# A gated delta-rule decoder layer on one Trainium2 core: output weights and roots earlier on GpSimd, the copy of the inverse on GpSimd, first odd units in other banks

## What is computed

```python
mixed = hidden_states @ w_qkv
z = (hidden_states @ w_z).reshape(B, S, HV, DV)
...
y = jax.lax.conv_general_dilated(x, conv_w, window_strides=(1,), padding=[(KCONV - 1, 0)], ...)
mixed = jax.nn.silu(y).transpose(0, 2, 1)
...
def step(Sm, inp):
    q_, k_, v_, g_, b_ = inp
    Sm = Sm * jnp.exp(g_)[..., None, None]
    kv = jnp.einsum('bhk,bhkv->bhv', k_, Sm)
    delta = (v_ - kv) * b_[..., None]
    Sm = Sm + jnp.einsum('bhk,bhv->bhkv', k_, delta)
    o = jnp.einsum('bhk,bhkv->bhv', q_, Sm)
    return (Sm, o)
...
og = o * jax.nn.silu(z)
var = jnp.mean(og * og, axis=-1, keepdims=True)
on = og * jax.lax.rsqrt(var + EPS) * norm_w
return on.reshape(B, S, VAL_DIM) @ w_out
```

## Time and profile before

| | us |
|---|---|
| median of three runs | 2256.93 |
| lowest and highest run | 2249.43, 2257.33 |
| profiled execution, its own time | 2255.11 |
| span of its instructions | 2253.2 |
| TensorE busy | 2091.6 (93%) |
| VectorE busy | 1711.3 (76%) |
| ScalarE busy | 1512.7 (67%) |
| GpSimd busy | 904.1 (40%) |

### The profile page before, as it was taken

The page is one execution under the profiler, slowest core; times in us unless marked ns, Lnnn a source line. Parts: engine busy times, 40 slices in busy tenths (PEclk is TensorE's granted clock), DMA queues, the critical chain, the costliest instruction groups (busy, mean ns, idle before and its releaser), DMA issues.

```text
span 2253.2 us, 49295 instructions
## 1 busy us (share of the span) xinstructions
PE 2091.6 (93%) x18636; PEld 1716.1 (76%) x18636; DVE 1711.3 (76%) x2944; ACT 1512.7 (67%) x3585; POOL 904.1 (40%) x714
## 2 busy tenths in 40 slices
PE   4659999999999999999999999999988899999998
PEld 4448888888888888888888888887776476666776
DVE  6789797887879788787977978787325777767665
ACT  4547777777777777777777677775767666565632
POOL 1534454444445445445535534532333123213232
PEclk8779999999999999999999999998999999999999
DMA  3432322322232332233233222212243012322232
GB/s 77 94 73 48 89 44 72 63 64 67 55 85 46 72 75 49 68 60 80 52 70 72 48 70 56 75 34 56 58 137 133 1 66 76 104 94 73 91 136 85
DMA packets 274633, 161.56 MB, mean 72 GB/s; under 512 B 209352, under 2 KB 246752, under 8 KB 269280
## 3 DMA queue, kind: packets, MB, share of 16 engines
q1 hardware_dynamic: 274400, 158.41, 27.6%
HBM read 122.43 MB, written 35.91 MB: 70 GB/s over the span
## 4 chain that ended last, share of the span: by engine, by line
issue 36%; POOL 26%; PE 23%; DVE 8%; ACT 4%; DMA 2%; SPq 2%; POOLq 0%; DVEq 0%; ACTq 0%
POOL SM L577 5%; POOL EB L493 5%; POOL Q L555 5%; PE ps L1739 4%; POOL SZ L579 3%; PE ps L1347 3%; POOL EB L497 3%; PE ps L1349 3%; PE ps L1348 3%; POOL WL L471 2%; POOL SM L585 2%; PE ps L1660 1%; ACT SC L856 1%; PE ps L1651 1%; PE ps L1480 1%
## 5 line engine op out<-in xcount | busy, mean ns | idle before, releaser
L909 DVE SCALAR_TENSOR_TENSOR A<-ps,CW,A 128x508 f32<-128x508 f32 (+2 forms) x768 | 515.9, 734 | 55.3 <-ACT A L671 50.1
L572 POOL TENSOR_SCALAR SM<-SM 128x8 f32<-128x8 f32 x64 | 12.6, 196 | 813.8 <-ACT DL L690 813.8
L1480 PE MATMUL ps<-WO,DL 128*128 128x256 f32 x1008 | 244.5, 394 | 39.5 <-POOL WO L484 24.5
L1480 PEld LDWEIGHTS ps<-WO,DL 128*128 128x128 f32 x1008 | 189.7, 194 | 74.5 <-POOL WO L484 26.4
L1347 PE MATMUL ps<-XH,WH 128*128 128x512 f32 x512 | 221.5, 433 | 26.7 <-DVE A L909 25.8
L1127 DVE TENSOR_TENSOR SZ<-SZ,ps 128x512 f32<-128x512 f32 x128 | 87.7, 687 | 201.5 <-PE ps L1514 201.4
L1349 PE MATMUL ps<-XH,WL 128*128 128x512 f32 x512 | 206.4, 403 | 0.0
L1348 PE MATMUL ps<-XL,WH 128*128 128x512 f32 x512 | 205.2, 401 | 0.0
L690 ACT ACTIVATE DL<-SZ 128x128 f32<-128x128 f32 x512 | 152.4, 298 | 38.5 <-PE ps L1514 28.8
L856 ACT ACTIVATE SC<-ps,A 128x128 f32<-128x128 f32 x512 | 141.7, 386 | 51.5 <-DVE A L1252 50.7
L1112 DVE TENSOR_TENSOR BP<-ps,EB 128x512 f32<-128x512 f32 x256 | 158.3, 681 | 3.3 <-ACT EB L665 3.3
(11 more groups left out here) (225 smaller groups left out, 5556.1 us busy)
## 6 DMA issues: line engine op xcount, KB each, us to landing
EB<-decay_rows SPq DMA_DIRECT2D x128, 256.0 KB, 4.7
WE<-expert_halves SPq DMA_DIRECT2D x32, 1024.0 KB, 5.1
x_blocks<-BP SPq DMA_DIRECT2D x256, 32.0 KB, 1.7
X<-x_blocks SPq DMA_DIRECT2D x16, 512.0 KB, 6.5
tt_blocks<-TI SPq DMA_DIRECT2D x16, 512.0 KB, 2.6
tn_blocks<-TM SPq DMA_DIRECT2D x16, 512.0 KB, 2.6
TTF<-tt_blocks SPq DMA_DIRECT2D x256, 32.0 KB, 1.9
expert_halves<-BP SPq DMA_DIRECT2D x8, 1024.0 KB, 5.8
```

Source lines behind the costliest of these rows:

```text
L909: dve.scalar_tensor_tensor(acc, ps(i, 0, [[128, 4], [1, 128 - s]]), at(CW, tile * 4 + 3 - s, [[1, 1]]), acc, ALU.mult, ALU.add).then_inc(s ...
L1480: t = pe.matmul(ps(7 - i, b * 256, [[1, 256]]), at(on_buf(k), (4 * i + 2 * b + v) * 128, [[1, 128]]), at(WO, v * 256, [[1, 256]]), start=( ...
```

## The change

Four things are changed.

1. `load_wo` and `scale_wo` of the next key head are called in ticks 4j (k % 4 == 3) and no longer in ticks 4j+1: on SyncE behind `load_rows`, on GpSimd behind `decay` and ahead of the norm of unit m.
2. The root of the keys' norms (L585, now L570) stands ahead of that norm as well, in the same tick as before.
3. The copy `TM<-TI` is taken off ScalarE and made by GpSimd's `tensor_copy` behind `decay`, in the same ticks 4j+3. The title's "moved within GpSimd's tick" holds for the root; the copy comes from another engine.
4. Units 1, 3, 5 and 7 project into banks 4 and 5. A projection in the first ticks waits for the taps of the unit two before, ScalarE does `kq_tap3(n + 1)` ahead of the `Silu` of unit n for n < 6, and three waits are adapted (the first projection on `ab`, `kq_tap3(6)` on the unit two before, the first transposes of values on the taps of unit 7).

```diff
@@ -217,6 +217,9 @@
         def kq_buf(n):
             return A2 if n < 6 and n % 2 else A1
 
+        def kq_bank(n):
+            return 4 if n < 8 and n % 2 else 0
+
@@ -392,8 +395,6 @@
                 for n in range(NT):
                     m, k = n - LAG3, n - LAG4
                     vn = m + 1
-                    if 0 < k < NSTEP and k % 4 == 0:
-                        load_wo(k // 4)
@@ -411,6 +412,8 @@
                         store_x(n)
                     if n + 3 < NSTEP:
                         load_rows(n + 3)
+                    if 0 <= k and k % 4 == 3 and k + 1 < NSTEP:
+                        load_wo(k // 4 + 1)
@@ -553,14 +556,24 @@
                         if n:
                             pool.wait_ge(sem["nq_mm"], n)
                         pool.tensor_tensor(at(Q2, 0, full), at(buf, 0, full), at(buf, 0, full), ALU.mult).then_inc(sem["sq"], 1)
-                    if 0 < k < NSTEP and k % 4 == 0:
-                        scale_wo(k // 4)
                     if EARLY - 1 <= n and n + 2 < NSTEP:
                         decay(n + 2)
                     if n == 5:
                         split_lo("v", W_V, 0)
                         split_lo("z", W_Z, 0)
                         scale_wo(0)
+                    if n % 4 == 0 and 4 <= n <= NSTEP:
+                        j = n // 4 - 1
+                        pool.wait_ge(sem["nk"], j + 1)
+                        if j >= 2:
+                            pool.wait_ge(sem["vv"], 4 * (4 * j - 4))
+                        pool.tensor_tensor(at(SM, C_SK + (j % 2) * 16, [[4, 4], [1, 4]]), at(SM, C_NK, [[4, 4], [1, 4]]),
+                                           at(SM, C_PH, [[0, 4], [1, 4]]), ALU.pow).then_inc(sem["sk"], 1)
+                    if 0 <= k and k % 4 == 3 and k + 1 < NSTEP:
+                        scale_wo(k // 4 + 1)
+                    if sv and vn % 4 == 0:
+                        pool.wait_ge(sem["inv"], INV_OPS * (vn // 4 + 1))
+                        pool.tensor_copy(at(TM, 0, [[1, 32], [32, 32]]), at(TI, 0, [[32, 32], [1, 32]])).then_inc(sem["tn"], 1)
@@ -577,13 +590,6 @@
...
                         pool.tensor_tensor(szp, szp, at(SM, C_RR, [[1, 8], [0, 128]]), ALU.mult).then_inc(sem["on"], 1)
-                    if n % 4 == 0 and 4 <= n <= NSTEP:
-                        j = n // 4 - 1
-                        pool.wait_ge(sem["nk"], j + 1)
-                        if j >= 2:
-                            pool.wait_ge(sem["vv"], 4 * (4 * j - 4))
-                        pool.tensor_tensor(at(SM, C_SK + (j % 2) * 16, [[4, 4], [1, 4]]), at(SM, C_NK, [[4, 4], [1, 4]]),
-                                           at(SM, C_PH, [[0, 4], [1, 4]]), ALU.pow).then_inc(sem["sk"], 1)
@@ -649,7 +655,7 @@
                     act.activation(at(WH, off, [[1, 512]]), at(WR, off, [[1, 512]]), ACT.Copy).then_inc(sem["hi_" + name], 1)
 
                 def kq_tap3(n):
-                    back = n - 2 if n < 6 else n - 1
+                    back = n - 2 if n <= 6 else n - 1
...
                     for i, tile in enumerate((HK + n // 4, n // 4)):
                         act.wait_ge(sem["kq_proj"], 2 * n + 1 + i)
-                        act.activation(at(kq_buf(n), i * 512, [[1, 512]]), ps(i), ACT.Copy,
+                        act.activation(at(kq_buf(n), i * 512, [[1, 512]]), ps(kq_bank(n) + i), ACT.Copy,
                                        scale=at(CW, tile * 4 + 3, [[1, 1]])).then_inc(sem["kq_tap3"], 1)
@@ -750,6 +756,8 @@
                                            scale=-1.0).then_inc(sem["u1_sb"], 1)
                     if s3 and m:
                         squares(m - 1, 1)
+                    if n < 6:
+                        kq_tap3(n + 1)
                     if s1:
                         act.wait_ge(sem["kq_conv"], 6 * n + 6)
@@ -772,10 +780,10 @@
                         u2_copy(m, 0)
                     if sv:
                         v_tap3(vn, 0)
-                    if n < EARLY:
+                    if n == 6:
                         kq_tap3(n + 1)
-                        if n == 2:
-                            split_hi("kq", W_KQ, 1)
+                    if n == 2:
+                        split_hi("kq", W_KQ, 1)
@@ -801,9 +809,6 @@
                         decay_exp(n + 1)
                     if s4 and k < NSTEP - 1:
                         on_T(k, 0)
-                    if sv and vn % 4 == 0:
-                        act.wait_ge(sem["inv"], INV_OPS * (vn // 4 + 1))
-                        act.activation(at(TM, 0, [[1, 32], [32, 32]]), at(TI, 0, [[32, 32], [1, 32]]), ACT.Copy).then_inc(sem["tn"], 1)
                     if s4 and k < NSTEP - 1:
                         on_T(k, 1)
...
-                def tap(name, n, buf, tiles, s):
...
-                        dve.scalar_tensor_tensor(acc, ps(i, 0, [[128, 4], [1, 128 - s]]), at(CW, tile * 4 + 3 - s, [[1, 1]]), acc,
+                        dve.scalar_tensor_tensor(acc, ps(bank + i, 0, [[128, 4], [1, 128 - s]]), at(CW, tile * 4 + 3 - s, [[1, 1]]), acc,
                                                  ALU.mult, ALU.add).then_inc(sem[name + "_conv"], 1)
...
                 def kq_tap(n, s):
-                    tap("kq", n, kq_buf(n), (HK + n // 4, n // 4), s)
+                    tap("kq", n, kq_buf(n), (HK + n // 4, n // 4), s, kq_bank(n))
@@ -1366,11 +1371,13 @@
                     for i in range(2):
                         if vn >= 0:
                             pe.wait_ge(sem["v_conv"], 6 * vn + 5 + i)
+                        elif n >= 2:
+                            pe.wait_ge(sem["kq_conv"], 6 * (n - 2) + 5 + i)
                         elif n:
-                            pe.wait_ge(sem["kq_conv"], 6 * (n - 1) + 5 + i)
+                            pe.wait_ge(sem["ab"], 4)
                         else:
                             pe.wait_ge(sem["x_lo"], 2)
-                        proj(i, W_KQ + 128 * i, n % 4).then_inc(sem["kq_proj"], 1)
+                        proj(kq_bank(n) + i, W_KQ + 128 * i, n % 4).then_inc(sem["kq_proj"], 1)
@@ -1616,6 +1623,8 @@
                         for b in range(4):
                             if b % 2 == 0 and s3:
                                 pe.wait_ge(sem["delta"], 2 * m + 1 + b // 2)
+                            elif b == 0:
+                                pe.wait_ge(sem["kq_conv"], 6 * 8)
                             for v in range(2):
                                 t = pe.transpose(ps(4 + b // 2, (b % 2) * 256 + v * 128, [[1, 128]]), at(A2, v * 512 + b * 128, [[1, 128]]), idn)
                             if b % 2:
```

1 line of the change is left out of this document (added).

## The result

The changed kernel takes 2264.4 us (median of 20 runs, 2254.2 to 2278.4), the kernel before 2256.6 (20 runs): a ratio of 1.0038, interval 1.0025 to 1.0050. The change makes the kernel slower by 8 us. I had forecast 2247 and a range from 2234 to 2261. The result lies 3 us above the range, and the time moved the other way.

What follows compares the result with a forecast made beforehand. TensorE, busy for 1172.36 of 1200 us in the body, was taken to bound the kernel. Terms -17.1 + 10.4 + 2.6 - 1.5 - 5.6 + 3.0 = -8.2 us against 2255.11 gave 2246.9; range 2234 to 2261.

Steps and rivals of the forecast that it cites:

- The wait for the weights, -17.1: Ticks 4j+5: with the scaling one tick earlier, TensorE's wait before L1480 goes, 13 x 1.31 = -17.1 us.
- Moving the root of L585 itself costs nothing: GpSimd, ticks 4j+5: the root stood behind L579 and goes into a stretch where GpSimd waited 14.87 us; no cost.
- The ports, +10.4: Ticks 4j+5: GpSimd's L579 and VectorE exclude each other, so L579 is late; 0.8 us a tick, 13 x 0.8 = +10.4.
- The scaling ahead of the norm: GpSimd, ticks 4j+5: waits for the weights' landing ahead of L572; L579 ends about 2.0 us later, 0.4 us remain.
- The copy, +2.6: Ticks 4j+3: GpSimd's copy takes 2.04 us, so TA reaches L1533 0.2 us later than before; 13 x 0.2 = +2.6.
- rival (a): Ticks 4j+3: the strided write is free on GpSimd, copy 1.04 us, the 0.65 is kept; -11, 2236; chance 0.16.
- (d): Rival, ticks 4j+3: a copy of about 2.5 us on GpSimd, 13 x 0.45 = +6, 2253; chance 0.11.
- The -1.5 of ticks 63 and 67: GpSimd has no unit to square or mask there, so the copy starts sooner and TensorE's waits are won: -1.5 us.
- The last load, -5.6: Tick 69: load issued in tick 68, so TensorE's 7.41 us wait ends sooner, released by ScalarE's L677; -5.6 us.
- The first ticks, +3 (bounds -2.5 and +6): Ticks 2 to 4: ScalarE's SiLU stands behind the taps, delaying L1583 and the next projection; banks give at most 0.85 a tick.
- the slower one that I wrote, a slow copy: Rival: the copy is a slow path on GpSimd; at 4 us it costs 25.5, giving 2272; chance 0.09.
- (b) or (c): Rivals: (b) ports don't matter, the 10.4 falls away, 2236.5, chance 0.13; (c) banks shorten first ticks, -2.5, 2241.5, chance 0.06.

Runs made afterwards that it cites:

- Experiment 5: Kernel before with the root of 16 elements (L585) alone moved ahead of the norm: 2254.6 us, ratio 0.9996.
- experiments 3 and 4: Changed kernel with the weights' load sooner, between load_ta and load_tt: 2267.6 us; the same with the root also back behind the norm: 2234.5 us.
- experiment 2: Changed kernel with the root put back behind the norm, all else as changed: 2276.1 us, ratio 1.0098.
- second profile: The changed kernel profiled once more with no edit: 2266.7 us, ratio 1.0057; the profiled execution has a span of 2263.5 us.
- experiment 6: Kernel before with the copy of the inverse alone moved from ScalarE to GpSimd behind the decays: 2253.5 us, ratio 0.9990.
- experiment 7: Kernel before with the first ticks alone changed (banks and ScalarE's order): 2260.5 us; with the banks alone: 2254.8 us.
- the two profiles: Two profiled executions of the unedited changed kernel: spans 2252.3 and 2263.5 us.
- the last version: Kernel before with weights loaded earlier and scaled behind the root, decays ahead of squares in odd ticks, inverse's copy on GpSimd: 2218.2 us, ratio 0.9840.

## Why the prediction was wrong, step by step

The step that failed is the account of the ticks 4j+1 behind the wait that went: the collision with VectorE was priced on GpSimd's side alone, and the root's move and the later scaling were followed on GpSimd's queue to L579 and no further. The body was to win 4.1 us from tick 9 to 61 and lost 7.4. Step by step:

- **The wait for the weights, -17.1:** right. L1480 no longer waits for them in ticks 4j+1.
- **"Moving the root of L585 itself costs nothing":** false, and one half of the failed step. I looked only at what stood behind the root on its own queue. Behind L579 it also left the ports free while L963 ran. Experiment 5 shows it by itself (1.42 to 3.08 us), experiments 3 and 4 as the difference of 33 us that it makes once the weights come early. Taking this half back alone doesn't mend the kernel (experiment 2, 2276.1), because of the other half, below.
- **The ports, +10.4:** the collision of L579 with L963 was foreseen, but priced on one side only, as lateness of L579. That side is there and smaller than I took: L1470 waits 3.4 us in ten periods of the second profile, 0.34 a period instead of 0.8. The other side, VectorE late, costs 14.2 us in the same stretch (L1352 and L1540), 1.4 a period. I had written that the two exclude each other, and did not ask who waits for VectorE. The race between the landing and L947, on which I based the 0.8, is real; it decides between the two kinds of tick.
- **The scaling ahead of the norm:** that it waits for the landing was right (13.28 us of idle time ended by the DMA). The lateness goes on to the squares and the mask, and ScalarE waits there; I followed the queue as far as L579 and no further. Experiment 2 shows that end: 2.38 us at L1629.
- **The copy, +2.6:** the price was right (2.07 us measured, 2.04 taken; neither the 1.04 of rival (a) nor the 2.5 of (d)), the wait named was not: no L1540 waits for `TA`. L1533 did not "want to start at 448.25", since ScalarE, held by the mask, holds TensorE for 0.62 us ahead of it. And `TA` is there 0.8 us sooner after the copy than I reckoned, since I took the longest of three landings. Net about 0; experiment 6 has -2 us with an interval from -4 to 0. The -1.5 of ticks 63 and 67 can't be read: the stretch from tick 61 to 69 varies more than that by itself.
- **The last load, -5.6:** right in kind, somewhat less in size. In tick 69 L1487 starts 4.5 us behind `on_tr` where L1480 started 9.1 behind it. TensorE still stands 2.8 us idle there: ScalarE's L683 comes 0.9 us later than I took it, behind a split of expert weights that waits for its DMA. And the 7.41 us of the kernel before was a long one; in the four kernels that leave this load in its place the wait is 5.5 to 6.7, so the gain is 2.7 to 4.6 us.
- **The first ticks, +3 (bounds -2.5 and +6):** right in sign, too small: +5.1 us alone (interval 3.2 to 7.2), +6.4 at tick 9 of the second profile. The later SiLU was seen. It starts the inverse 0.7 us late in experiment 7 and 1.5 and 2.2 in the two profiles, not 3; most of the rest are collisions inside the inverse, which I took for a stretch that absorbs things. That +3 lies near +5 is in part luck: the mechanism was half of it.
- **The rivals:** the slower one that I wrote, a slow copy, did not happen. Nor did (b) or (c). The true one was not on the list. Of the signs that I had named, the wait of L1470 and the price of the copy came, the wait for `TA` didn't. Term by term, from before to the second profile: +6.4 to tick 9 where I had +3; +7.4 to tick 61 where I had -17.1 + 10.4 + 2.6 = -4.1; +1.0 where I had -1.5; -4.5 where I had -5.6. Sum +10.3 against -8.2.

What stays open: why the same load lands after 5.4 us in one tick and after 7.4 in another, and why behind `load_rows` it takes over twice as long as ahead of `load_tt`. Of the last version's 10 us over the one with the copy on ScalarE, the profiles show 10.8 from tick 9 to 61 and 2.5 in the first ticks, against 3.5 lost from tick 61 to 69. The 10.8 are 0.83 a period, and the waits for L813 were 0.7, so they fit the copy; the other two I can't assign.
